# Group norm statistics and transposes of an attention kernel moved to token order, with x turned by DMA

## The chip, the cores and the metric

The kernel runs on one core of a Trainium2 chip. The metric is the device time of one execution in microseconds (us). TensorE (PE), VectorE (DVE), ScalarE (ACT), GpSimd (POOL) and SyncE (SP) run their own instruction streams in order and wait for one another through semaphores.

## The reference

x has shape 64 x 14 x 14 x 768 in fp32: 64 images of 196 tokens with 768 channels. What is computed is

```
gn    = (x - mean) / sqrt(var + 1e-5)        # per image, 32 groups of 24 channels over all 196 tokens
qkv   = gn @ qkv_w.T + qkv_b,  q += gn @ la_q.T @ lb_q.T,  v += gn @ la_v.T @ lb_v.T
attn  = softmax(q * scale @ k.T + rel_h(q) + rel_w(q))       # 12 heads of 64, per image
out   = x + (attn @ v) @ proj_w.T + proj_b
```

## The kernel before

A first block (`prepare`) loads the weights, folds the low-rank parts in, turns them on TensorE and splits each into an fp16 high and low part. The second block (`attend`) works on 32 pairs of images. A pair is 392 tokens in four tiles of 98. Products of fp32 accuracy are made of three fp16 matmuls (high x high, high x low, low x high).

All engines follow orders written out by hand: `PE_ORDER`, `ACT_ORDER`, `DVE_ORDER`, `POOL_ORDER`, `SP_ORDER`. One pass over an order is called a row of the pipeline here; in row q an entry `each(kind, old, k...)` is the step `kind` of pair q - old, so that -1 is the next pair, -2 the one after it, and 1 and 2 are earlier ones. `sequence` unrolls the orders over all rows from -2 on. A row has twelve units, each begun by S (scores of head pair k//2 of image k%2):

- Q, K, V: 18 matmuls of 392 columns each (L556) into a bank of `ring`, read by ACT (high part) and DVE (low part). Y is the same for the output projection (L623), Z turns the result back to token order on PE (L629), DVE adds x into `y_sb` (L803).
- S: scores (L599). DVE takes the row maximum (L769, L773), ACT the exponentials (N, L682), DVE and ACT scale and split them (N and T, L777, L781, L789, L690), SP turns `split` into `turned` by a DMA transpose (SP's T, L528) and `v_split` into `v_tok` (VT, L523), PE multiplies (P, L613). `S` of the next unit waits for the exponentials of the last.
- R: relative position terms (L578, L756, L762), copied by SP's CA and CB.
- X: PE turns x, fp32, from 98 tokens x 768 channels to 128 channels x 392 tokens (L637, 24 transposes for a pair); ACT copies each of the six results to `xT` (L708), DVE takes `bn_stats` of each half (L808).
- M and G: `bn_aggr` (L813, L814), a mean over the channels of each group by a matmul with `gmean` (L642), the spread of the channel means, a second matmul, and `pow` on POOL (L722).
- H and L: DVE normalises `xT` (L833), ACT writes `xn_hi` (L712), DVE `xn_lo` (L839). Q waits for `xn_lo` in three steps.
- LD: ACT's queue loads x of a later pair (L653). LY loads x again for the sum and ST stores, by way of `YS` = 3 slots of `y_sb`.

`ring` has five banks given out in the order of use (`ring_plan`): a user of a bank waits until the fifth user before it has been read. ACT and DVE begin `attend` with a wait for two memsets on POOL (L716, L717).

Of the kernel before, what the change touches and what calls it, by code (L numbers as in the profile page):

```python
# [35 lines left out]
GP = C // GROUPS // CT  # L36
# [3 lines left out]
YS = 3  # L40
# [12 lines left out]
def each(kind, old, *ks):  # L53
    return [(kind, old, k) for k in ks]
# [6 lines left out]
    + each("S", 0, 3) + each("P", 0, 1) + each("K", 0, 2) + each("Y", 1, 2) + each("Z", 1, 1)  # L61
    + each("S", 0, 4) + each("P", 0, 2) + each("V", 0, 2) + each("Z", 1, 2) + each("Q", -1, 0)
    + each("S", 0, 5) + each("P", 0, 3) + each("K", 0, 3) + each("Q", -1, 1)
    + each("S", 0, 6) + each("P", 0, 4) + each("V", 0, 3) + each("Q", -1, 2, 3)
    + each("S", 0, 7) + each("P", 0, 5) + each("K", 0, 4) + each("Q", -1, 4)
    + each("S", 0, 8) + each("P", 0, 6) + each("Q", -1, 5) + each("V", 0, 4)
    + each("S", 0, 9) + each("P", 0, 7) + each("R", -1, 0) + each("K", 0, 5) + each("R", -1, 1) + each("Y", 1, 3)
    + each("S", 0, 10) + each("P", 0, 8) + each("R", -1, 2, 3, 4) + each("V", 0, 5) + each("Y", 1, 4) + each("Z", 1, 3)
    + each("S", 0, 11) + each("P", 0, 9) + each("K", -1, 0) + each("X", -2, 0, 1, 2) + each("Y", 1, 5) + each("Z", 1, 4))


def soft(u):
# [4 lines left out]
    each("Y", 2, 5) + each("X", -1, 3) + each("N", 0, 0) + each("X", -1, 4, 5) + each("T", 0, 0)  # L77
    + each("V", 0, 0) + each("P", 1, 11) + each("N", 0, 1) + each("K", 0, 1) + each("T", 0, 1)
    + each("Y", 1, 0) + soft(2) + each("V", 0, 1)
    + each("Y", 1, 1) + each("H", -1, 0) + each("P", 0, 1) + each("N", 0, 3) + each("K", 0, 2) + each("T", 0, 3)  # L80
    + each("H", -1, 1)
    + each("Y", 1, 2) + each("H", -1, 2) + soft(4) + each("V", 0, 2)
    + each("Q", -1, 0) + each("P", 0, 3) + each("N", 0, 5) + each("K", 0, 3) + each("T", 0, 5)
    + each("Q", -1, 1) + soft(6) + each("V", 0, 3) + each("LD", -2, 0) + each("Q", -1, 2)
    + each("Q", -1, 3) + each("P", 0, 5) + each("N", 0, 7) + each("K", 0, 4) + each("T", 0, 7)
    + each("Q", -1, 4) + soft(8) + each("Q", -1, 5)
    + each("V", 0, 4) + each("P", 0, 7) + each("R", -1, 0) + soft(9) + each("K", 0, 5) + each("R", -1, 1)
    + each("Y", 1, 3) + each("R", -1, 2) + each("N", 0, 10) + each("R", -1, 3, 4) + each("T", 0, 10) + each("V", 0, 5)
    + each("Y", 1, 4) + each("P", 0, 9) + each("N", 0, 11) + each("K", -1, 0) + each("T", 0, 11)
    + each("X", -2, 0, 1, 2))  # L90
# [40 lines left out]

PER_PAIR = {"Q": 6, "K": 6, "V": 6, "R": RCH, "Y": 6, "Z": 6, "X": 6, "G": 2}
# [21 lines left out]
def build(nc, x, qkv_w, qkv_b, proj_w, proj_b, la_q, lb_q, la_v, lb_v, rel_h, rel_w, out, pairs=PAIRS):  # L154
    V, A, T, G = nc.vector, nc.scalar, nc.tensor, nc.gpsimd
    with ExitStack() as keep:
# [12 lines left out]
        gmean = sb(keep, "gmean", [128, 128], F32)  # L169
# [18 lines left out]
def prepare(nc, g):  # L188
# [5 lines left out]
    with ExitStack() as own:  # L194
# [65 lines left out]
        def _(pool):  # L260
            count = [0]

            def step(ins):
# [7 lines left out]

            step(G.memset(gmean[:, :], 1.0 / GP))
            view = gmean[:, :].rearrange("p (a b) -> p a b", b=GP)
            step(G.affine_select(out=view, in_=view, compare_op=ALU.is_ge, fill=0.0, base=0,
                                 pattern=[[-GP, 128 // GP], [0, GP]], channel_multiplier=1))
            step(G.affine_select(out=view, in_=view, compare_op=ALU.is_ge, fill=0.0, base=GP - 1,
                                 pattern=[[GP, 128 // GP], [0, GP]], channel_multiplier=-1))

# [23 lines left out]
        def _(dve):  # L302
# [76 lines left out]
            for part, table in enumerate((rt_hi, rt_lo)):  # L379
                for head in range(2):  # L380
                    for at in (32 * head, 32 * head + 16):
                        rows = slice(64 * head, 64 * head + 64)
                        V.tensor_copy(table[rows, :, :, at:at + H],
                                      rel16[rows, part, :, :].rearrange("p a (r k) -> p a r k", r=H))

        @block.tensor
        def _(pe):
# [19 lines left out]
            pe.wait_ge(pool_step, 7)  # L407
# [7 lines left out]
            for n, (grp, t, j0) in enumerate(turns):  # L415
                if n >= 4:
                    pe.wait_ge(lo_made, n - 3)
                for i in range(3):
                    if grp < 3:
                        src = stage[:, j0 + i, :].rearrange("p (a b) -> p b a", b=CT)[:, t, :]  # L420
                    else:
                        src = stage[:, j0 + i, 128 * t:128 * t + 128]
                    last = T.transpose(ring[:, n % 4, 128 * i:128 * i + 128], src, ident[:, :])
                last.then_inc(turned, 1)


def attend(nc, g, pairs):
# [9 lines left out]
    with ExitStack() as own:  # L437
        S = lambda name, shape, dt: sb(own, name, shape, dt)
        sem = lambda name: own.enter_context(nc.semaphore(name))
        xT = S("xT", [128, CT, NT], F32)  # L440
        xn_hi = S("xn_hi", [128, 2, CT, NT], F16)
        xn_lo = S("xn_lo", [128, 2, CT, NT], F16)

# [418 lines left out]
```

## Time and profile before

| | us |
|---|---|
| time, median of 3 runs | 3375.34 (3371.14 to 3375.82) |
| the profiled execution, its own time | 3373.03 |
| its span in the trace | 3371.3 |
| PE busy | 3297.2 |
| DVE busy | 2528.2 |
| ACT busy | 2098.2 |
| PE work on the chain that ended last | 94% of the span |

A matmul's duration includes its way through the array, and successive matmuls overlap, so what a group costs is read from the starts of its first matmul and of the next group's, and not from the mean. The same holds in smaller measure for DVE and ACT, where an instruction starts some 0.08 us before the last one ends. The mean granted TensorE clock of the execution was 0.991.

### The profile page before, as it was taken

What the parts mean: (1) busy time and instruction counts of PE and PEld (TensorE: products, weight loads), DVE (VectorE), ACT (ScalarE), POOL (GpSimd) and SP (SyncE); (2) the same over time, 40 slices, a digit from 0 to 9 for tenths busy, and PEclk for the clock granted to TensorE, in tenths of its full rate; (3) what the DMA queues carried; (4) which work ended last, traced back from release to release, by engine and by line L of the source; (5) the groups of instructions that cost most, each with busy time, mean ns of one, the idle gap of its engine ahead of it and who ended that gap; (6) DMA issues with size and microseconds to landing.
All of it is one profiled execution on the core that took longest, in us unless ns stands there. A gap on an engine that the chain in (4) does not pass through costs nothing.

```text
span 3371.3 us, 80148 instructions
## 1 busy us (share of the span) xinstructions
PE 3297.2 (98%) x31984; PEld 2130.7 (63%) x31984; DVE 2528.2 (75%) x5970; ACT 2098.2 (62%) x5651; POOL 35.8 (1%) x65
## 2 busy tenths in 40 slices
PE   7689999999999999999999999999999999999998
PEld 4456666666666666666666666666666666666665
DVE  7577777777777777777777777777777777777764
ACT  2466666666666666666666666666666666666664
POOL 0000000000000000000000000000000000000000
PEclk9799999999999999999999999999999999999999
DMA  3145664555555556565555555555565555565554
GB/s 128 42 96 109 120 122 103 115 113 112 118 121 107 113 112 114 116 121 107 110 116 113 112 123 118 101 117 111 110 127 120 100 118 108 111 126 122 103 106 105
DMA packets 1091412, 376.13 MB, mean 112 GB/s; under 512 B 916696, under 2 KB 1071320, under 8 KB 1091040
## 3 DMA queue, kind: packets, MB, share of 16 engines
q1 hardware_dynamic: 1075206, 333.63, 49.8%
q10 hardware_dynamic: 15834, 37.37, 3.9%
q8 instruction: 254, 4.16, 0.5%
q14 instruction: 118, 0.97, 0.1%
HBM read 86.60 MB, written 38.54 MB: 37 GB/s over the span
## 4 chain that ended last, share of the span: by engine, by line
PE 94%; DVE 2%; ACT 1%; issue 0%; DMA 0%; POOL 0%; SPq 0%; POOLq 0%; DVEq 0%
PE ring L556 51%; PE ring L623 17%; PE score L599 9%; PE o_ps L613 7%; PE ring L578 3%; PE ring L637 3%; PE ring L629 3%; ACT prob L682 1%; PE ring L642 0%; PE ring L563 0%; DVE split L789 0%; DVE row_max L769 0%; DVE rel_sb L762 0%; DVE split L781 0%; DVE rel_sb L756 0%
## 5 line engine op out<-in xcount | busy, mean ns | idle before, releaser
L556 PE MATMUL ring<-xn_hi,w_hi 128*128 128x392 f16 x3456 | 1143.2, 331 | 4.8 <-DVE xn_lo L839 4.6
L556 PE MATMUL ring<-xn_lo,w_hi 128*128 128x392 f16 x3456 | 1139.8, 330 | 0.0
L556 PE MATMUL ring<-xn_hi,w_lo 128*128 128x392 f16 x3456 | 1139.3, 330 | 0.5 <-issue 0.5
L682 ACT ACTIVATE prob<-score,neg_max,exp_scale 98x196 f32<-98x196 f32 x1536 | 769.8, 511 | 252.9 <-DVE neg_max L773 245.4
L769 DVE TENSOR_REDUCE row_max<-score 98x4 f32<-98x784 f32 x384 | 373.3, 972 | 273.2 <-PE score L599 272.1
L789 DVE SCALAR_TENSOR_TENSOR split<-prob,row_inv,split 98x196 f16<-98x196 f32 x1536 | 545.0, 417 | 7.8
L556 PEld LDWEIGHTS ring<-xn_hi,w_hi 128*128 128x128 f16 x3456 | 342.3, 99 | 260.7 <-issue 7.7
L556 PEld LDWEIGHTS ring<-xn_hi,w_lo 128*128 128x128 f16 x3456 | 338.8, 98 | 237.9 <-issue 3.6
L556 PEld LDWEIGHTS ring<-xn_lo,w_hi 128*128 128x128 f16 x3456 | 338.9, 98 | 208.3 <-issue 1.9
L623 PE MATMUL ring<-o_hi,w_hi 128*128 128x392 f16 x1152 | 380.2, 330 | 1.4 <-DVE o_lo L798 1.4
L623 PE MATMUL ring<-o_lo,w_hi 128*128 128x392 f16 x1152 | 379.8, 330 | 0.0
L623 PE MATMUL ring<-o_hi,w_lo 128*128 128x392 f16 x1152 | 379.6, 330 | 0.0
L690 ACT ACTIVATE split<-prob,row_inv 98x196 f16<-98x196 f32 x768 | 310.3, 456 | 52.9 <-DVE row_inv L777 52.1
L682 ACT ACTIVATION_READ_ACCUMULATOR prob<-score,neg_max,exp_scale 98x1 f32 x1536 | 306.2, 199 | 0.0
L658 ACT ACTIVATE q_hi<-ring,bias 128x392 f16<-128x392 f32 x192 | 112.1, 584 | 297.8 <-PE ring L556 297.8
L777 DVE RECIPROCAL row_inv<-row_sum 98x4 f32<-98x4 f32 x384 | 68.0, 177 | 290.6 <-ACT prob L682 290.6
L613 PE MATMUL o_ps<-turned,v_tok 98*64 98x196 f16 x4608 | 269.5, 252 | 4.0 <-DMA turned<-split 4.0
L701 ACT ACTIVATE yT<-ring,bias,y_scale 128x392 f32<-128x392 f32 x192 | 130.1, 678 | 220.6 <-PE ring L623 220.6
L599 PE MATMUL score<-k_hi,q_hi 64*98 64x196 f16 x1536 | 205.7, 264 | 19.7 <-DVE k_lo L736 12.3
L781 DVE TENSOR_SCALAR split<-prob,row_inv 98x196 f16<-98x196 f32 x768 | 213.0, 320 | 14.3 <-DVE row_inv L777 0.8
L613 PEld LDWEIGHTS o_ps<-turned,v_tok 98*64 98x64 f16 x4608 | 184.8, 109 | 56.1 <-DMA turned<-split 4.3
L697 ACT ACTIVATE o_hi<-o_ps,bias 128x392 f16<-128x392 f32 x192 | 112.7, 587 | 141.3 <-PE o_ps L613 141.3
(118 smaller groups left out, 4896.7 us busy)
## 6 DMA issues: line engine op xcount, KB each, us to landing
y_sb<-in_x SPq DMA_DIRECT2D x192, 196.0 KB
out<-y_sb SPq DMA_DIRECT2D x192, 196.0 KB
x_sb<-in_x ACTq DMA_DIRECT2D x31, 1176.0 KB
rel_q<-rel_sb SPq DMA_DIRECT2D x128, 122.5 KB, 2.4
stage<-in_L_conv_qkv_w SPq DMA_DIRECT2D x3, 2304.0 KB, 15.4
turned<-split SPq DMA_TRANSPOSE x384, 4.2
rel_q<-rel_sb SPq DMA_DIRECT2D x128, 24.5 KB, 1.9
v_tok<-v_split SPq DMA_TRANSPOSE x192, 3.4
```

What stands on the lines that cost most here:

```text
L556: last = T.matmul(ring[:, bank, 0:NT], w[:, c, 128 * j:128 * j + 128], xx[:, par, c, :], start=(c == 0 and part == 0), stop=(c == CT - 1 a ...
L599: last = T.matmul(score[0:HALF, head, to], stat[rows, qs], kk[rows, :], start=(part == 0), stop=(part == 3))
L613: last = T.matmul(o_ps[rows, c0:c0 + TOK], v_tok[0:HALF, hp % 2, vv, 2 * image + kh, rows], turned[0:HALF, image, pp, head, :, kh, 0:HALF] ...
L623: last = T.matmul(ring[:, bank, 0:NT], w[:, c, 128 * j:128 * j + 128], oo[:, par, c, :], start=(c == 0 and part == 0), stop=(c == HP - 1 a ...
L658: last = A.activation(to, ring[:, bank, 0:NT], ACT.Identity, bias=bias[:, j:j + 1])
L682: last = A.activation(prob[:, head, half, :], score[0:HALF, head, TOK * half:TOK * half + TOK], ACT.Exp, bias=neg_max[:, k % 2, i:i + 1], ...
L690: last = A.activation(split[0:HALF, k % 2, 0, 0, half, :, 0:HALF], prob[:, 0, half, :].rearrange("p (a k) -> p a k", a=2), ACT.Copy, scale ...
L697: A.activation(o_hi[:, par, hp, :], o_ps[:, 0:NT], ACT.Identity, bias=bias[:, 2 * CT + hp:2 * CT + hp + 1]).then_inc(o_hi_made, 1)
L701: A.activation(yT[:, k % 2, :], ring[:, bank, 0:NT], ACT.Identity, bias=bias[:, 3 * CT + k:3 * CT + k + 1], scale=y_scale[:, :]).then_inc( ...
L769: V.tensor_reduce(row_max[:, k % 2, :], score[0:HALF, :, 0:2 * TOK].rearrange("p a (b k) -> p a b k", b=2), AX.X, ALU.max).then_inc(row_ma ...
L781: last = V.tensor_scalar(split[0:HALF, k % 2, 0, 1, half, :, 0:HALF], prob[:, 1, half, :].rearrange("p (a k) -> p a k", a=2), row_inv[:, k ...
L789: last = V.scalar_tensor_tensor(split[0:HALF, k % 2, 1, head, half, :, 0:HALF], prob[:, head, half, :].rearrange("p (a k) -> p a k", a=2), ...
```

## The change

The group norm is worked out in token order (98 tokens in the partitions, channels along the free dimension), on `x_sb` itself. `A` sums x over groups (two `tensor_reduce`, each of two token tiles, 1536 elements), `G 0` is a matmul with a constant matrix that gives the mean to all partitions, `B` subtracts it in place, `U` squares on ACT, `D` sums the squares, `G 1` turns and sums them to one column of 64, POOL takes the power -0.5, `E` puts the result on a diagonal, `G 2` gives it to all partitions, `H` multiplies. `I` (ACT) and `L` (DVE) write the fp16 high and low part to `xs`, and SP turns `xs` into `xn` by four DMA transposes for a pair (`XT`). X on PE, its copies on ACT and its statistics are gone. `squares` and the `qw` buffers share the memory of `xs`. `YS` falls to 2, `yT` to one buffer, the tables of R to 32 columns, and the channel order of the weights is now the plain one. The wait of ACT and DVE for all cleared buffers is replaced by one wait for each buffer at its first use.

```diff
-YS = 3
+YS = 2
 PE_ORDER = (
-    each("S", 0, 0) + each("P", 1, 10) + each("Z", 2, 5) + each("X", -1, 3, 4, 5) + each("V", 0, 0)
-    + each("S", 0, 1) + each("P", 1, 11) + each("K", 0, 1) + each("Y", 1, 0) + each("G", -1, 0)
-    + each("S", 0, 2) + each("P", 0, 0) + each("G", -1, 1) + each("V", 0, 1) + each("Y", 1, 1) + each("Z", 1, 0)
...
+    each("S", 0, 0) + each("P", 1, 10) + each("Z", 2, 5) + each("V", 0, 0) + each("K", 0, 1)
+    + each("S", 0, 1) + each("P", 1, 11) + each("G", -1, 1) + each("V", 0, 1) + each("G", -1, 2) + each("Y", 1, 0)
+    + each("S", 0, 2) + each("P", 0, 0) + each("K", 0, 2) + each("Y", 1, 1) + each("Z", 1, 0)
+    + each("S", 0, 3) + each("P", 0, 1) + each("Y", 1, 2) + each("Z", 1, 1) + each("V", 0, 2)
+    + each("S", 0, 4) + each("P", 0, 2) + each("Z", 1, 2) + each("K", 0, 3) + each("Q", -1, 0)
...
+    + each("S", 0, 8) + each("P", 0, 6) + each("G", -2, 0) + each("Q", -1, 4, 5)
+    + each("S", 0, 9) + each("P", 0, 7) + each("K", 0, 5) + each("R", -1, 0) + each("Y", 1, 3) + each("R", -1, 1)
     + each("S", 0, 10) + each("P", 0, 8) + each("R", -1, 2, 3, 4) + each("V", 0, 5) + each("Y", 1, 4) + each("Z", 1, 3)
-    + each("S", 0, 11) + each("P", 0, 9) + each("K", -1, 0) + each("X", -2, 0, 1, 2) + each("Y", 1, 5) + each("Z", 1, 4))
+    + each("S", 0, 11) + each("P", 0, 9) + each("K", -1, 0) + each("Y", 1, 5) + each("Z", 1, 4))
 ACT_ORDER = (
+    each("Y", 2, 5) + each("U", -1, 1) + soft(0) + each("V", 0, 0)
+    + each("K", 0, 1) + each("P", 1, 11) + soft(1) + each("V", 0, 1)
+    + each("Y", 1, 0) + each("I", -1, 0) + each("N", 0, 2) + each("K", 0, 2) + each("T", 0, 2) + each("I", -1, 1)
...
+    + each("Q", -1, 0) + each("P", 0, 3) + soft(5) + each("V", 0, 3) + each("LD", -2, 0)
...
+    + each("Y", 1, 4) + each("U", -2, 0) + each("P", 0, 9) + each("N", 0, 11) + each("K", -1, 0) + each("T", 0, 11))
 DVE_ORDER = (
+    each("S", 0, 0) + each("D", -1, 1) + soft(0) + each("V", 0, 0) + each("Z", 2, 4, 5)
+    + each("S", 0, 1) + each("G", -1, 1) + each("K", 0, 1) + each("P", 1, 11) + each("E", -1, 0) + soft(1)
+    + each("G", -1, 2) + each("V", 0, 1) + each("H", -1, 0)
+    + each("S", 0, 2) + each("H", -1, 1) + each("N", 0, 2) + each("K", 0, 2) + each("T", 0, 2) + each("L", -1, 0)
+    + each("S", 0, 3) + each("Z", 1, 0) + each("P", 0, 1) + each("L", -1, 1) + soft(3)
...
+    + each("S", 0, 6) + each("Q", -1, 1) + each("N", 0, 6) + each("K", 0, 4) + each("T", 0, 6) + each("A", -2, 0)
+    + each("S", 0, 7) + each("Q", -1, 2) + each("P", 0, 5) + soft(7) + each("V", 0, 4) + each("A", -2, 1)
+    + each("S", 0, 8) + each("Q", -1, 3) + each("G", -2, 0) + soft(8) + each("Q", -1, 4) + each("B", -2, 0)
...
     + each("S", 0, 11) + each("Z", 1, 3) + each("P", 0, 9) + each("N", 0, 11) + each("K", -1, 0) + each("T", 0, 11)
-    + each("X", -2, 0, 1, 2))
+    + each("B", -2, 1) + each("D", -2, 0))
 SP_ORDER = (
     each("ST", 2, 4) + each("CB", 0, 0) + each("T", 0, 0)
-    + each("VT", 0, 0) + each("LY", 1, 0) + each("ST", 2, 5) + each("T", 0, 1) + each("LY", 1, 1)
...
+    + each("VT", 0, 0) + each("ST", 2, 5) + each("LY", 1, 0) + each("T", 0, 1)
+    + each("VT", 0, 1) + each("LY", 1, 1) + each("XT", -1, 0) + each("T", 0, 2)
+    + each("XT", -1, 1, 2) + each("ST", 1, 0) + each("XT", -1, 3) + each("T", 0, 3) + each("LY", 1, 2)
...
+                elif kind == "XT":
+                    part, image = k // 2, k % 2
+                    wait(sp, xs_lo_made if part else xs_hi_made, 2 * p + image + 1)
+                    sp.sem_inc(sp_go, 1)
+                    sp.dma_start_transpose(xn[:, p % 2, part, 2 * image:2 * image + 2].rearrange("p b c r -> p (b c) r"),
+                                           xs[0:ROWS, part, 2 * image:2 * image + 2].rearrange("r b c -> r (b c)")
+                                           ).then_inc(xn_in, 16)
...
-                        if kind == "Q" and k == 0 and c % 2 == 0:
-                            wait(pe, xn_lo_made, 3 * p + c // 2 + 1)
+                        if kind == "Q" and k == 0 and c == 0:
+                            wait(pe, xn_in, 64 * p + 64)
...
         def _(act):
-            act.wait_ge(split_zeroed, 2)
...
+                elif kind == "U":
+                    wait(act, centred, 2 * p + k + 1)
+                    if p == 0 and k == 0:
+                        act.wait_ge(xs_zeroed, 1)
+                    wait(act, done["R"], RCH * p)
+                    A.activation(squares[:, two], x_sb[:, two, :], ACT.Square).then_inc(squared, 1)
...
         def _(pool):
+            G.memset(minus_half[:, :], -0.5).then_inc(minus_half_made, 1)
+            G.memset(ones[:, :], 1.0).then_inc(ones_made, 1)
+            G.memset(xs[:, :, :, :].rearrange("p a b c -> p (a b c)"), 0.0).then_inc(xs_zeroed, 1)
+            G.memset(v_split[:, :, :, :, :].rearrange("p s a b k -> p (s a b k)"), 0.0).then_inc(v_zeroed, 1)
             G.memset(split[:, :, :, :, :, :, :].rearrange("r s a b c d k -> r (s a b c d k)"), 0.0).then_inc(split_zeroed, 1)
...
+                elif kind == "A":
+                    if k == 0:
+                        wait(dve, x_in, 16 * p + 16)
+                    two = slice(2 * k, 2 * k + 2)
+                    V.tensor_reduce(sums[:, k, :], x_sb[:, two, :].rearrange("p b (g c) -> p g b c", c=GP),
+                                    AX.XY, ALU.add).then_inc(summed, 1)
...
+                elif kind in ("B", "H"):
+                    wait(dve, read["G"], 3 * p + (1 if kind == "B" else 3))
+                    by_group = x_sb[:, 2 * k:2 * k + 2, :].rearrange("p b (g c) -> p b g c", c=GP)
+                    of = (mean if kind == "B" else rstd)[:, k:k + 1, :]
+                    V.tensor_tensor(by_group, by_group, of.unsqueeze(3).broadcast_to([HALF, 2, GROUPS, GP]),
+                                    ALU.subtract if kind == "B" else ALU.mult
+                                    ).then_inc(centred if kind == "B" else normed, 1)
```

In `prepare`, two of POOL's three instructions that make `gmean` are gone, and `rt_hi` and `rt_lo` are half as large.

## Rows read from the trace of the kernel before

**Rows 1.** The page: busy time of each engine, share of the span, instructions
```profile
PE 3297.2 (98%) x31984; PEld 2130.7 (63%) x31984; DVE 2528.2 (75%) x5970; ACT 2098.2 (62%) x5651; POOL 35.8 (1%) x65
```

**Rows 2.** Busy time by stretch, one row of the pipeline: us, each engine (instructions), PEclk, DMA share, GB/s
```profile
2090.08:2190.56 100.48, 100.48 (x995) 65.03 (x993) 76.82 (x183) 64.67 (x176) 0.69 (x1) 1.00 0.54 114
```

**Rows 3.** Timeline of PE in one row: start us, us, line, operation, tiles
```profile
2146.35 1.75 PE L637 MATMUL ring<-ident,x_sb 98*128 98x98 f32 x12
2147.93 0.33 PE L623 MATMUL ring<-o_hi,w_hi 128*128 128x392 f16 x1
...
2165.45 0.28 PE L642 MATMUL ring<-mean_var,gmean 128*128 128x2 f32 x2
2165.66 0.29 PE L599 MATMUL score<-k_hi,q_hi 64*98 64x196 f16 x2
...
2166.47 0.70 PE L613 MATMUL o_ps<-turned,v_tok 98*64 98x196 f16 x12
```

**Rows 4.** Groups by line and shape, whole execution: busy us, mean ns | idle before
```profile
L401 PE MATMUL lora_ps<-la,lbT 4*128 4x384 f32 x48 | 31.4, 849 | 9.8 <-DVE lbT L324 7.1 <-DVE stage L334 2.7
L808 DVE BATCH_NORM_STATS2 stats<-xT 128x6 f32<-128x196 f32 x384 | 112.9, 350 | 18.1 <-ACT xT L708 18.1
L839 DVE TENSOR_TENSOR xn_lo<-xT,xn_hi 128x784 f16<-128x784 f32 x96 | 87.6, 968 | 0.0
L833 DVE TENSOR_SCALAR xT<-xT,mean,rstd 128x392 f32<-128x392 f32 x192 | 83.4, 477 | 0.9 <-POOL rstd L722 0.9
L316 DVE TENSOR_REDUCE mx<-stage 128x1 f32<-128x4608 f32 x2 | 9.9, 4942 | 0.0
L712 ACT ACTIVATE xn_hi<-xT 128x784 f16<-128x784 f32 x96 | 80.9, 845 | 9.2 <-DVE xT L833 9.2
```

**Rows 5.** Timeline of DVE around the end of unit 11
```profile
2143.74 0.96 DVE L769 TENSOR_REDUCE row_max<-score 98x4 f32<-98x784 f32 x1
...
2147.13 0.18 DVE L777 RECIPROCAL row_inv<-row_sum 98x4 f32<-98x4 f32 x1 [1.04 <-ACT prob L682]
...
2148.35 1.41 DVE L789 SCALAR_TENSOR_TENSOR split<-prob,row_inv,split 98x196 f16<-98x196 f32 x4
2149.68 1.68 DVE L808 BATCH_NORM_STATS2 stats<-xT 128x6 f32<-128x196 f32 x6
```

**Rows 6.** Timeline of SP's queue in units 0 and 1: issue start us, us
```profile
2154.23 0.33 SPq L533 DMA_DIRECT2D out<-y_sb  x1
2154.67 2.43 SPq L505 DMA_DIRECT2D rel_q<-rel_sb  x4
2158.91 2.33 SPq L528 DMA_TRANSPOSE turned<-split  x1
2161.44 1.24 SPq L523 DMA_TRANSPOSE v_tok<-v_split  x1
```

**Rows 7.** The page: DMA issues, median us from issue to landing last
```profile
turned<-split SPq DMA_TRANSPOSE x384, 4.2
v_tok<-v_split SPq DMA_TRANSPOSE x192, 3.4
```

**Rows 8.** The chain of waits at the start of the main block: start us, us
```profile
89.69 3.51 POOL split L716
93.20 1.75 POOL v_split L717
...
106.18 20.75 PE ring L556 x108
...
129.36 0.16 PE ring L563
...
2098.28 9.06 PE ring L556 x54
```

**Rows 9.** Line L653, the loads of x: issue ns min/median/max, first and last start
```profile
L653 ACTq DMA_DIRECT2D x_sb<-in_x x31: 323/323/340, 115.0 to 3106.9; - x31
```

**Rows 10.** DMA from 120 to 125 us, GB/s in 40 equal slices
```profile
GB/s 295 270 270 221 98 98 49 25 0 0 0 0 0 0 0 0 0 0 0 0 0 0 0 0 0 0 0 0 0 0 0 0 0 0 0 0 0 0 0 0
```

More of the change, by code:

```diff
@@ L76 @@
 ACT_ORDER = (
[L77 to L89, printed above, removed]
@@ L270, in _ @@
                                  pattern=[[-1, 128]], channel_multiplier=1))
[L272 to L277, printed above, removed]
+            step(G.memset(gmean[:, :], 1.0 / (GP * TOK)))
             step(G.memset(pick[:, :, :], 0.0))
@@ L418, in _ @@
                 for i in range(3):
[L419 to L423, printed above, removed]
+                    last = T.transpose(ring[:, n % 4, 128 * i:128 * i + 128],
+                                       stage[:, j0 + i, 128 * t:128 * t + 128], ident[:, :])
                 last.then_inc(turned, 1)
@@ L577, in _ @@
                                             "p (g i w) -> p g i w", i=n_rows, w=W)[:, :, i, :]
-                                    last = T.matmul(cols, tab[rows, ax, row, 32 * head:32 * head + 32], mov,
+                                    last = T.matmul(cols, tab[rows, ax, row, :], mov,
                                                     start=(part == 0), stop=(part == 2))
@@ L718, in _ @@
-            G.memset(minus_half[:, :], -0.5).then_inc(minus_half_made, 1)
             pool.wait_ge(minus_half_made, 1)
             for kind, p, k in sequence(POOL_ORDER, pairs):
-                wait(pool, read["G"], 2 * p + 2)
-                G.tensor_tensor(rstd[:, :], var_eps[:, :], minus_half[:, :], ALU.pow).then_inc(rstd_made, 1)
+                wait(pool, read["G"], 3 * p + 2)
+                G.tensor_tensor(inv_dev[:, :], var_eps[:, :], minus_half[:, :], ALU.pow).then_inc(inv_dev_made, 1)
@@ new lines, in _ @@
+                elif kind == "A":
+                    if k == 0:
+                        wait(dve, x_in, 16 * p + 16)
+                    two = slice(2 * k, 2 * k + 2)
+                    V.tensor_reduce(sums[:, k, :], x_sb[:, two, :].rearrange("p b (g c) -> p g b c", c=GP),
+                                    AX.XY, ALU.add).then_inc(summed, 1)
+                elif kind == "D":
+                    wait(dve, squared, 2 * p + k + 1)
+                    two = slice(2 * k, 2 * k + 2)
+                    V.tensor_reduce(sums[:, k, :], squares[:, two].rearrange("p b (g c) -> p g b c", c=GP),
+                                    AX.XY, ALU.add).then_inc(summed, 1)
+                elif kind == "G" and k == 1:
+                    wait(dve, done["G"], 3 * p + 2)
+                    V.tensor_scalar(var_eps[:, :], ring[0:2 * GROUPS, bank, 0:1], EPS, None,
+                                    ALU.add).then_inc(read["G"], 1)
+                elif kind == "E":
+                    wait(dve, inv_dev_made, p + 1)
+                    V.tensor_scalar(diagonal[:, :], ident[0:2 * GROUPS, 0:2 * GROUPS], inv_dev[:, :], None,
+                                    ALU.mult).then_inc(diagonal_made, 1)
+                elif kind == "G":
+                    wait(dve, done["G"], 3 * p + k + 1)
+                    to = mean if k == 0 else rstd
+                    V.tensor_copy(to[:, :, :].rearrange("p n g -> p (n g)"),
+                                  ring[0:HALF, bank, 0:2 * GROUPS]).then_inc(read["G"], 1)
+                elif kind in ("B", "H"):
[5 more added lines that the diff above has]
+                                    ).then_inc(centred if kind == "B" else normed, 1)
```

195 lines of the change are left out of this document (82 added, 113 removed).

## The prediction

> **What bounds the kernel now.** I read the page's busy times first: PE 3297.2 of 3371.3 us, DVE 75% [rows 1]. A share says little, so I cut out one row of the pipeline: in the 100.48 us from one S 4 to the next PE is busy for all 100.48, DVE for 76.82, ACT for 64.67, at full clock, with the DMA engines 0.54 busy [rows 2]. In this steady part, some 30 rows, any time taken off PE is gained until another wait opens; time put on DVE costs nothing until it makes PE wait. Start and end are different: there PE waits for chains, so they are worked out apart.
>
> **PE in a steady row.** X leaves: the first twelve transposes start at 2146.35 and Y at 2147.93, so 1.58 for half a pair and 3.17 for a pair (the other half is alike) [rows 3]. The mean duration of a transpose would say twice as much; the starts count. The two G matmuls leave: 2165.45 to 2165.66 is 0.21 each, 0.42 together [rows 3]. Three come. G 1 has one column: 0.21. G 0 and G 2 have 64 columns, in fp32, which takes two instructions; L401 shows 31.4/48 = 0.654 us for 384 columns, 1.70 ns a column [rows 4], so 0.21 + 62 x 1.70 x 2 ns = 0.42 each. Together 1.05; no row shows this form, so the bounds are 0.63 (columns hidden) and 1.7 (twice the column price and a cold array). I take 1.05. The sum for a pair: -3.17 - 0.42 + 1.05 = -2.54. The moving operand of Q, K, V now lies in four runs of 98 instead of one of 392; P already reads runs of 98 at its normal pace, so nothing. Some 29.5 pairs have their X on a full PE (pair 0 and half of pair 1 fall in the start): **-75 us**, bounds -67 to -87.
>
> **DVE in a steady row.** Passes of 98 x 1536: the reduction of 4608 takes 4.94 and L839, with 784, takes 0.97 [rows 4], so 1.04 ns an element and 0.97 + 0.78 = 1.75, of which the next instruction hides some 0.08: 1.7. There are ten (A, B, D, H, L two each): 17.0, and 0.6 for G and E. Out go the statistics (112.9/32 = 3.5), H (83.4/32 = 2.6), L (87.6/32 = 2.7) [rows 4] and about 1.4 of aggregates and small steps: 10.2. So 76.8 + 7.4 = 84 of 98. ACT: U and I, 1536 elements, four times 0.85 + 0.63 = 1.48 by L712 [rows 4], 5.9 in and as much out. Neither is the bound by its sum; what matters is the order.
>
> **Where DVE can make PE wait.** A unit costs PE 0.81 for S and 0.63 for P, so 1.5 with the changeover, and 9.06/3 = 3.02 for each group of 18 matmuls [rows 8]. From the start of the maximum to the end of the exponentials is 2147.13 - 2143.74 = 3.4 [rows 5], so S of the next unit, 7.3 to 8.1 later, leaves DVE some 3 us of lateness for nothing. I went through the new orders unit by unit with these prices.
> - Unit 10: the four R steps (7 us of DVE) end with V 5 some 1.7 after S 11 starts.
> - Unit 11: max, Z, P, N, K, T end at S 11 + 7.8; then B 1 and D 0, at the end of the row, 11.2. PE needs 8.1 for the unit, so DVE enters the next row 3.1 late, the maximum of S 0 runs to 4.2, the exponentials to 6.5. S 1 is due at 8.1: no wait.
> - Unit 0: D 1 lies under the exponentials (ready at 5.9), then N, T, V, and Z 4 at 9.7, Z 5 at 10.3. PE reaches V 1 at 9.8, whose bank is that of Z 4: no wait, by 0.1. G 2 waits for E (pow on POOL 0.75 behind G 1): E is done at S 1 + 4.7, just when PE has finished V 1.
> - SP: ST 4 stands ahead of CB, T 0 and VT 0. Before, Z 4 was read 2.6 after S 0, and ST left at 2154.23; CB takes 2.43, T 0 was issued at 2158.91, VT 0 at 2161.44 [rows 6], with P 0 at 2166.47 [rows 3]. Now ST 4 leaves at 9.7, CB ends at 12.6, T 0 is issued to 14.2 or 15.0 (1.5, or the 2.33 of this row), VT 0 lands 3.4 later [rows 7], at 17.5 to 18.4. P 0 is due at 2 x 8.1 + 0.8 = 17.0. So **P of unit 0 waits for `v_tok`**, 0.4 to 1.4; I take 0.8. For 30 rows **+24 us**, bounds 0 (DVE 1 us earlier than I think) and 2 a row.
> - Units 2 and 3: H 0, I 0, H 1, I 1, L 0, L 1 end at S 3 + 5.5. XT lies between VT and T in size (12 blocks of 128 columns against 8 and 16), so 3.8 to land; the fourth lands near S 3 + 9.5, Q 0 is due at S 3 + 13.2. XT 0 stands ahead of T 2 on SP, but I 0 is early. No wait, by some 3.7.
> - Unit 6: LD is issued 2 us before S 6 and needs 6 (below); A 0 comes at S 6 + 6.9, cover 2 to 3. If it is gone, S 7's maximum, queued behind A 0, still has 3 us.
>
> The Trainium skill, in "VectorE: DVE Perf Modes", section "The three transpose paths", gives 1309 ns for a 128x128 block turned by DMA and 390 ns on TensorE, and advises TensorE where PSUM will do as the target. It speaks against this change. The rows do not bear the figure out: `turned`, sixteen blocks, lands 4.2 us after its issue [rows 7], where the page would make it 21.
>
> **The start.** Before, POOL's memset of `split` begins at 89.69, and ACT and DVE wait for it and the next one; Q starts at 106.18 [rows 8]. Now the first pair's chain is serial: from 89.7 A A 3.4; G 0 with a cold array and its copy 1.2; B B 3.4; D D 3.4 (U beside them); G 1, epsilon, pow, E, G 2, copy 3.2; H H L L 6.8; the last XT 1.0 + 3.8 to land: 115.9. That is +9.7. The wait that goes is worth nothing: `xs`, 6144 elements at 3.51/4096 us, is clear at 95.2, the first U is due at 96.1. Then Q to R, 23.2 before (129.36 - 106.18): G 0 of pair 1 now stands between Q 3 and Q 4, and wants its x. LD was issued at 115.0 [rows 9] and its data ended near 121.0 [rows 10], 6 us. Now it goes at Q + 5.7, x is there at Q + 12.0, A, Q 2, A end at 16.5, Q 5 is done at 23.1, R starts at 25.5: +2.3. The first full row lacks P, Y and Z of earlier pairs and was held by DVE and by two places where PE did two or three jobs in one unit; by the same sums it falls from 95.7 to 88.1: -7.6, of which -12 to 0 is possible. Two instructions less on POOL before the first DVE step: -1.2. Together **+3 us**, bounds -8 to +15.
>
> **The end.** With two slots of `y_sb`, Z 2 of the last pair waits for ST 0 to land and LY 2 after it, and Z 5 for ST 3: some 3 us each beyond PE's pace, the last one seen in full. **+3 us**, bounds 0 to 6.
>
> **The sum.** -75 + 24 + 3 + 3 = -45 against 3373.03, the profiled execution: 3328. The median of the runs shown is 2.3 higher: 3330.
>
> **The rivals.**
> 1. No new wait: Z 4 is read a microsecond earlier, or `v_tok` lands sooner. For it: the margins at V 1, G 2 and P 0 are all within 1 us, less than my error over twenty steps. -75 + 6: 3304.
> 2. The waits of units 0 to 2 are larger, 1.3 to 2.2 a row, as lateness of DVE adds to all three. For it: D, B and A are forms of which no row shows one (four dimensions, runs of 24). 3304 + 30 x 1.3 to 2.2 = 3343 to 3370. Against: DVE idles 14% of the row and catches up by unit 4.
> 3. Slower: B and H, whose two inputs are both fp32 in SBUF, one of them a broadcast, run at half the pace, 3.3 instead of 1.7. The nearest row, L839, has an fp32 and an fp16 input at 1.04 ns an element and speaks against it. Then Z 4 comes at 11.3: V 1 waits 1.5, P 0 another 0.9, Q 0 some 0.6: 3.0 a row, 3304 + 90 = 3394. It decides from a wait of 2.2 a row on; any lateness of DVE of that size does the same.
> 4. The crossbar turns `xs` slowly. It would work through `xn_in`: by [rows 7] the longest median is 4.2 for sixteen blocks, and Q 0 has 3.7 us of cover beyond 3.8; at 10 us to land, more than twice any row here, Q 0 waits 2.5 a row, 3304 + 75 = 3379. By the figure of the Trainium skill, "VectorE: DVE Perf Modes", "The three transpose paths", twelve blocks would land after 15.7 us, an estimate that the row above denies.
>
> **How the numbers follow.** My forecast 0.40; rival 1 0.25; rival 2 0.20; rival 3 0.13; rival 4 0.02. A measurement of this kernel can tell 0.2%, about 7 us, from no change, so "same" is 3368 to 3382. Faster: 0.40 + 0.25 + 0.17 = 0.82; same 0.05 (the end of rival 2 and part of 4); slower 0.13. The range takes in the forecast and rivals 1 and 2 with the bounds of start and price of G: 3290 to 3368, leaving out 0.17.
>
> **What would show it.** A row of the pipeline 98.7 long (97.9 without the new wait); no PE line for x; G at 1.0 a pair; ten DVE passes near 1.7; DVE 84 a row; PE's o_ps waiting for `v_tok` once a row, some 0.8; Q's first matmul at 115 to 116, and no steady wait on `xn`; the last Z behind LY. I am wrong if the passes take much over 1.7, or if PE waits for `xn` or for exponentials in every row.

## The result, and the profile after

The kernel after the change takes 3381.8 us (median, 3373.48 to 3395.74) beside 3374.54 for the kernel before: a ratio of 1.0025, 95% interval 1.0018 to 1.0033. It is slower by a quarter of a per cent, where 3330 and a gain of 1.3% were forecast. The profiled execution spans 3380.6 us, 9.3 more than before.

The page of after, busy times, answers [rows 1]:

```profile
PE 3218.0 (95%) x31280; PEld 2005.9 (59%) x31280; DVE 2755.3 (82%) x5490; ACT 2125.4 (63%) x5491; POOL 35.2 (1%) x65
```

PE does 79.2 us less and the kernel is no faster: PE now waits. Where it waits is in PE's waits from 1000 to 3000 us, twenty rows of the pipeline (us in total, times, longest us):

```profile
PE o_ps L611 <- issue: 20.0, 18, 3.7
PE o_ps L611 <- DMA turned<-split: 15.2, 8, 2.8
PE ring L554 <- DVE y_sb L815: 3.9, 11, 0.4
PE ring L639 <- DVE sums L821: 3.3, 20, 0.2
```

The busy time by stretch of after, columns as in [rows 2], two thousand microseconds of the steady part, then 8.2 us behind the longest wait, 7.1 us behind a wait of 2.05 and 8.3 us behind one of 2.69:

```profile
1000.00:2000.00 1000.00, 976.26 (x9665) 609.94 (x9665) 834.24 (x1670) 650.62 (x1687) 5.42 (x10) 0.99 0.65 127
2000.00:3000.00 1000.00, 979.77 (x9707) 612.39 (x9704) 838.77 (x1680) 655.16 (x1700) 5.41 (x10) 1.00 0.66 128
...
1973.80:1978.00 4.20, 4.14 (x22) 2.31 (x23) 0.89 (x4) 0.84 (x4) 0.00 (x0) 0.50 1.02 222
1978.00:1982.00 4.00, 4.00 (x21) 2.14 (x20) 0.91 (x3) 1.53 (x4) 0.00 (x0) 0.79 0.25 55
...
2076.90:2084.00 7.10, 7.09 (x52) 4.36 (x52) 5.11 (x11) 5.08 (x13) 0.00 (x0) 1.00 1.00 209
...
2775.70:2784.00 8.30, 8.26 (x41) 4.49 (x42) 2.70 (x7) 3.27 (x12) 0.00 (x0) 0.63 0.82 179
```

The two lines of `o_ps` (L611) make 35.2 us in twenty rows. 32.2 of them are P of unit 0, 1.61 a row, where 0.8 was forecast; the other 3.0 are six waits at P 10 of the pair before, just behind S 0; waits of that kind stay when P of unit 0 no longer waits (below). From one row maximum of S 0 to the next, 29 rows took 2915.9 us before (241.89 to 3157.82) and 2907.1 after (256.17 to 3163.26): 100.55 and 100.24 a row. The steady part gained 0.31 a row instead of 1.8; the start, up to the first of these maxima, lost 14.3; what comes behind the last of them lost 3.9. -8.8 + 14.3 + 3.9 = +9.4, the 9.3 of the spans but for rounding.

One ordinary row and the worst one, PE's timeline of after (start us, us, the wait ahead in brackets, with what ended it), answering [rows 3]:

```profile
1420.13 0.36 PE L639 MATMUL ring<-sums,gmean 98*98 98x64 f32 x2 [0.17 <-DVE sums L821]
...
1453.85 0.29 PE L597 MATMUL score<-k_hi,q_hi 64*98 64x196 f16 x2
...
1463.76 0.50 PE L554 MATMUL ring<-xn,w_hi 128*128 128x392 f16 x2 [0.36 <-DVE y_sb L815]
...
1472.70 0.70 PE L611 MATMUL o_ps<-turned,v_tok 98*64 98x196 f16 x12 [1.58 <-DMA turned<-split]
...
1973.86 1.19 PE L611 MATMUL o_ps<-turned,v_tok 98*64 98x196 f16 x12 [3.68 <-issue]
```

SP's queue ahead of the P at 1472.70, answering [rows 6], and DVE's reading of Z 4 and Z 5 that lets ST 4 go:

```profile
1463.72 0.33 SPq L531 DMA_DIRECT2D out<-y_sb  x1
1464.17 2.43 SPq L496 DMA_DIRECT2D rel_q<-rel_sb  x4
1466.71 1.55 SPq L519 DMA_TRANSPOSE turned<-split  x1
1468.45 1.84 SPq L514 DMA_TRANSPOSE v_tok<-v_split  x1
```

```profile
1457.01 0.96 DVE L779 TENSOR_REDUCE row_max<-score 98x4 f32<-98x784 f32 x1
...
1463.02 1.28 DVE L815 TENSOR_TENSOR y_sb<-ring,y_sb 98x512 f32<-98x512 f32 x2
```

Against S 0 at 1453.85 the steps read: DVE takes the maximum at +3.2, Z 4 is read at +9.8, ST 4 leaves at +9.9, CB is through at +12.75, T 0 is issued at +12.9, VT 0 at +14.6, P starts at +18.85 and would have started at 17.3. The bracket names `turned`; it and `v_tok` are both awaited there, and both stand behind ST 4 on SP. By the trace T 0 landed at 1471.83 and VT 0 at 1472.61, 0.09 before P began, so `v_tok` is what P waited for.

The second price is in the last four rows of the stretches. Behind the wait of 3.68 PE ran 4.2 us at a granted clock of 0.50, that is 1.2 GHz, and the twelve P matmuls took 1.19 instead of 0.70. Rows with a wait near 1.1 are 99.3 long; the row with 3.68 is 104.7 long (1956.06 to 2060.74), so 2.6 us of wait more made the row 5.4 longer. Six of the 29 rows take 101.9 to 104.7: their waits at P are 1.97 to 3.68, and behind each of them a stretch stands below full clock. The others take 97.9 to 100.4; two of these have a wait of 2.05 and kept the full clock (the stretch from 2076.90).

### The profile page after: what moved, and what is told of

Read it like the earlier page. It is cut to its first block, busy times and chain, and to the rows that moved or that the text cites. A ratio compares the mean times of both kernels' runs of the same rounds, so it can differ in the third digit from the quotient of the medians.

```text
span 3380.6 us, 78578 instructions
## 1 busy us (share of the span) xinstructions
PE 3218.0 (95%) x31280; PEld 2005.9 (59%) x31280; DVE 2755.3 (82%) x5490; ACT 2125.4 (63%) x5491; POOL 35.2 (1%) x65
## 4 chain that ended last, share of the span: by engine, by line
PE 57%; DVE 23%; ACT 9%; issue 4%; DMA 4%; SPq 2%; POOL 0%; ACTq 0%; DVEq 0%; POOLq 0%
PE ring L554 31%; PE ring L621 11%; ACT prob L686 6%; DVE split L801 6%; PE score L597 5%; PE o_ps L611 4%; DVE sums L821 3%; DMA turned<-split 3%; DVE row_max L779 2%; PE ring L576 2%; DVE x_sb L845 2%; DVE split L793 2%; PE ring L627 2%; DVE rel_sb L772 1%; DVE sums L826 1%
## 5 line engine op out<-in xcount | busy, mean ns | idle before, releaser
L554 PE MATMUL ring<-xn,w_hi 128*128 128x392 f16 x6912 | 1720.6, 330 | 17.7 <-DMA xn<-xs 11.8
L554 PE MATMUL ring<-xn,w_lo 128*128 128x392 f16 x3456 | 1137.7, 329 | 0.0
L554 PEld LDWEIGHTS ring<-xn,w_hi 128*128 128x128 f16 x6912 | 645.5, 97 | 493.2 <-issue 14.1
L554 PEld LDWEIGHTS ring<-xn,w_lo 128*128 128x128 f16 x3456 | 333.1, 96 | 246.1 <-issue 6.1
L611 PE MATMUL o_ps<-turned,v_tok 98*64 98x196 f16 x4608 | 270.8, 252 | 55.0 <-DMA turned<-split 29.4
L611 PEld LDWEIGHTS o_ps<-turned,v_tok 98*64 98x64 f16 x4608 | 187.0, 109 | 108.6 <-DMA turned<-split 33.6
L597 PE MATMUL score<-onehot,rel_q 64*98 64x196 f16 x1536 | 191.4, 245 | 0.0
L597 PE MATMUL score<-k_lo,q_hi 64*98 64x196 f16 x1536 | 191.3, 245 | 0.0
L597 PE MATMUL score<-k_hi,q_lo 64*98 64x196 f16 x1536 | 191.1, 245 | 0.0
```

The lines of the kernel that those rows point to most:

```text
L554: last = T.matmul(ring[:, bank, 0:NT], w[:, c, 128 * j:128 * j + 128], xn[:, par, xx, :, c, 0:HALF], start=(c == 0 and part == 0), stop=(c ...
L597: last = T.matmul(score[0:HALF, head, to], stat[rows, qs], kk[rows, :], start=(part == 0), stop=(part == 3))
L611: last = T.matmul(o_ps[rows, c0:c0 + TOK], v_tok[0:HALF, hp % 2, vv, 2 * image + kh, rows], turned[0:HALF, image, pp, head, :, kh, 0:HALF] ...
```

## The experiments

**One order on SP.** T 0 and VT 0 go ahead of ST 4 and CB; nothing else of the kernel after changes.

```
-    each("ST", 2, 4) + each("CB", 0, 0) + each("T", 0, 0)
-    + each("VT", 0, 0) + each("ST", 2, 5)
+    each("T", 0, 0)
+    + each("VT", 0, 0) + each("ST", 2, 4) + each("CB", 0, 0) + each("ST", 2, 5)
```

> The changed kernel with SP's row begun by T 0 and VT 0, with ST 4 and CB behind them. Queue theory (P of unit 0 waits because ST 4, now late, holds CB, T 0 and VT 0 back on SP): T 0 and VT 0 are issued as soon as unit 0 is split, some 3 us earlier, PE's wait for o_ps and the cold stretch behind it go, a row falls from 100.24 to some 97.7 us and the kernel to about 3306. Crossbar theory (the four more transposes of a pair slow v_tok and turned down, whatever stands ahead of them): the wait stays within 0.5 us of what it is, 3370 or more.

Measured: 3323.13, ratio 0.9855 (0.984 to 0.987). PE's waits from 1000 to 3000 us:

```profile
PE ring L554 <- DVE y_sb L815: 4.5, 13, 0.4
PE ring L639 <- DVE sums L821: 3.7, 21, 0.2
PE o_ps L611 <- issue: 1.5, 5, 0.4
```

The wait at `o_ps` falls from 35.2 to 1.5, PE is busy for 1989.5 of 2000 us, and a row takes 98.19 (1339.42 to 1437.61). The 1.5 are all waits of that P 10: P of unit 0 didn't wait once. The order of SP's queue alone holds 57 us (1.0025 against 0.9855). The transposes themselves, XT among them, are unchanged here, so a slow crossbar isn't the cause. The time is 17 above the queue theory's 3306. That number took rows of 97.7, and the 29 rows take 98.21 on average, which is 15 of the 17.

**The same from DVE's side.** SP keeps its order, Z 4 is read ahead of D 1.

```
-    each("S", 0, 0) + each("D", -1, 1) + soft(0) + each("V", 0, 0) + each("Z", 2, 4, 5)
+    each("S", 0, 0) + each("Z", 2, 4) + each("D", -1, 1) + soft(0) + each("V", 0, 0) + each("Z", 2, 5)
```

> The changed kernel with Z 4 moved on DVE from the end of unit 0 to just behind its row maximum, ahead of D 1; SP's order untouched. Queue theory: ST 4 leaves some 4.5 us earlier, the wait for o_ps goes as in the reordered queue, about 3306. Theory that DVE's fullness (84 us a row) is what PE waits for: its work is the same, only its order differs, so most of the wait stays, 3360 or more.

Measured: 3315.61, ratio 0.9833 (0.9818 to 0.9848). DVE and SP of one row (the maximum of S 0 is at 1434.36, S 0 itself at 1431.21):

```profile
1435.49 0.69 DVE L815 TENSOR_TENSOR y_sb<-ring,y_sb 98x512 f32<-98x512 f32 x1
```

```profile
1436.20 0.33 SPq L531 DMA_DIRECT2D out<-y_sb  x1
1436.64 2.47 SPq L496 DMA_DIRECT2D rel_q<-rel_sb  x4
1440.07 1.55 SPq L519 DMA_TRANSPOSE turned<-split  x1
1441.81 1.80 SPq L514 DMA_TRANSPOSE v_tok<-v_split  x1
```

ST 4 leaves 5.0 after S 0 instead of 9.9, VT 0 is issued at +10.6 instead of +14.6, and P of unit 0 doesn't wait in any of the twenty rows; the 1.8 us left at `o_ps` are waits of P 10. V 1 no longer waits for the bank of Z 4 either (3.9 in twenty rows before this edit, none now). A row is 97.74 (1336.62 to 1434.36) and 97.93 on average over the 29, 2.6 less than before the change; DVE does all its new passes, 855 of 1000 us. So DVE's greater load costs nothing here; its order did.

**The same wait put into the kernel before.** ST 4 also waits until DVE has read V 0 of the row.

```
                 elif kind == "ST":
                     wait(sp, read["Z"], 6 * p + k + 1)
+                    if k == 4 and p + 2 < pairs:
+                        wait(sp, read["V"], 6 * (p + 2) + 1)
```

> The kernel before with one more wait: ST 4 on SP also waits until V 0 of the row has been read, some 6 us later than Z 4. No DMA transpose is added and DVE does the same work. Queue theory: VT 0 goes out near 2166 instead of 2161.4, lands 3 to 4 us after P of unit 0 is due, and 30 rows pay that and a cold clock behind it: 3374 + 100 to 190, 3474 to 3564. Crossbar theory and DVE theory: no change, within 10 us of the kernel before.

Measured: 3490.93, ratio 1.0353 (1.0335 to 1.037). PE's waits and busy time from 1000 to 3000 us:

```profile
PE o_ps L615 <- DMA turned<-split: 32.1, 12, 3.2
PE o_ps L615 <- issue: 15.5, 7, 2.5
```

```profile
1000.00:2000.00 1000.00, 975.80 (x9571) 627.14 (x9570) 735.98 (x1740) 621.33 (x1677) 6.41 (x9) 0.99 0.55 109
```

The path from ST 4 to P is the same in the kernel before, without x turned by DMA and with DVE 74% busy. Neither of the other two theories allows this: both forecast no change. A row takes 104.18 on average over the 29 (102.6 to 107.1 from the second on), 3.6 more than in before. Of these 2.4 are PE's wait at P of unit 0; the other 1.2, by subtraction, is the same work done more slowly behind the waits. It isn't spread evenly. In 12 rows the granted clock stayed full, and they are longer by their wait alone; in 16 the clock fell (0.968 to 0.984 over the row), and they are 1.7 to 3.3 longer beyond their wait. The length of the wait doesn't tell them apart: waits of 2.10 to 2.62 are in the first group, 2.14 to 3.48 in the second, and the same wait of 2.15 stands in a row of 102.66 and in one of 105.81.

**Two transfers moved off VT 0's heels.** The wait varies from row to row between 0.8 and 3.7, and I suspected ST 5 and LY 0, 196 KB each, issued right behind VT 0.

```
-    + each("VT", 0, 0) + each("ST", 2, 5) + each("LY", 1, 0) + each("T", 0, 1)
-    + each("VT", 0, 1) + each("LY", 1, 1)
+    + each("VT", 0, 0) + each("T", 0, 1)
+    + each("VT", 0, 1) + each("ST", 2, 5) + each("LY", 1, 0) + each("LY", 1, 1)
```

> The kernel after, with one change of SP's order: ST 5 (196 KB out) and LY 0 (196 KB in), which SP issues 1.9 and 2.6 us behind VT 0, go behind T 1 and VT 1. ST 4 still stands ahead of CB, T 0 and VT 0, so P of unit 0 can start no earlier than in the best rows of after. Queue theory alone (the wait is the time at which VT 0 is issued, and the scatter from 1.1 to 3.7 comes from elsewhere): P(0,0) waits 1.76 a row as in after, 3382 (3376 to 3387). Queue plus crowding (the two bulk transfers issued behind VT 0 share the DMA engines with it, and this makes it land up to 6.4 instead of 3.8 us after its issue; behind a long wait PE's clock falls): the wait is 1.1 in every row, no row runs at 1.2 GHz, rows of 99.2 instead of 100.2, 30 x 0.9 = 27 less: 3355 (3348 to 3362).

Measured: 3387.86, ratio 1.0044 (1.0028 to 1.0061). The waits from 1000 to 3000 us:

```profile
PE o_ps L611 <- issue: 19.1, 17, 2.0
PE o_ps L611 <- DMA turned<-split: 15.9, 7, 2.7
```

35.0 against 35.2 (33.8 against 32.2 for P of unit 0 alone), and the time is just above the 3376 to 3387 of the first theory: the two transfers aren't what makes the landing scatter. The traces show what goes with it. These are lines of the DMA view of after from T 0's issue to its landing, with VT 0's time to landing, in the row with the wait of 3.68 (1965.76 to 1971.79) and, behind the dots, in one with a wait of 1.09 (1367.38 to 1371.51):

```profile
q14 instruction: 1, 0.01, 1.7%
q8 instruction: 1, 0.02, 1.0%
v_tok<-v_split SPq DMA_TRANSPOSE x1, 6.3
...
q1 hardware_dynamic: 2411, 0.63, 77.9%
v_tok<-v_split SPq DMA_TRANSPOSE x1, 3.7
```

In the second stretch the queues that the profile names `instruction` move nothing. In 28 rows of after, T 0 lands 4.11 to 4.22 us after its issue in the 14 in which no packet of these queues starts while it is under way, and 4.66 to 6.34 in the 14 with one or two (8 or 16 KB each); VT 0 lands behind T 0 each time. In e5 the same split gives 4.09 to 4.19 and 4.38 to 6.29. So the lateness is there at T 0 already, ahead of ST 5 and LY 0. No run took these packets away: that they are the cause isn't shown. The scatter matters only where VT 0 is issued late: with either order edit P of unit 0 waited in none of the twenty rows.

**The start: cleared buffers.** In the kernel before, each cleared buffer is waited for at its first use, and `minus_half` and `v_split` are cleared ahead of `split`.

```
-            act.wait_ge(split_zeroed, 2)
-            dve.wait_ge(split_zeroed, 2)
...
+            G.memset(minus_half[:, :], -0.5).then_inc(minus_half_made, 1)
+            G.memset(v_split[:, :, :, :, :].rearrange("p s a b k -> p (s a b k)"), 0.0).then_inc(v_zeroed, 1)
+            G.memset(split[:, :, :, :, :, :, :].rearrange("r s a b c d k -> r (s a b c d k)"), 0.0).then_inc(split_zeroed, 1)
```

> The kernel before with one part of the change alone: each cleared buffer is waited for at its first use, and split is cleared last. ACT's first copy of x no longer waits until 94.98 but for PE alone, near 91. If the start is one serial chain, it shortens by about 4 us, 3370; if something else ends later in the start, 0.

Measured: 3373.65, ratio 1.0002 (0.9993 to 1.0011): nothing. POOL's timeline shows why:

```profile
91.24 3.52 POOL L721 MEMSET split<- 112x4096 f16 x1
101.75 0.73 POOL L725 TENSOR_TENSOR rstd<-var_eps,minus_half 128x2 f32<-128x2 f32 x1 [7.00 <-issue]
```

The last step of the statistics began at 97.24, 4.4 earlier than in before, but POOL's pow began 7.0 behind its last memset all the same. The kernel after has this too, and its memsets are 5.2 longer:

```profile
95.24 3.51 POOL L729 MEMSET split<- 112x4096 f16 x1
105.61 0.59 POOL L733 TENSOR_TENSOR inv_dev<-var_eps,minus_half 64x1 f32<-64x1 f32 x1 [6.86 <-issue]
```

Its operand was ready at 99.95. So pow comes 5.7 late, and clearing `xs` (5.2 of POOL's time) costs the start some 5.2 of it, by way of POOL and not by the wait at U, where I had looked.

**Pow ahead of two memsets.** From here on with Z 4 ahead of D 1.

```
-            G.memset(v_split[:, :, :, :, :].rearrange("p s a b k -> p (s a b k)"), 0.0).then_inc(v_zeroed, 1)
-            G.memset(split[:, :, :, :, :, :, :].rearrange("r s a b c d k -> r (s a b c d k)"), 0.0).then_inc(split_zeroed, 1)
...
                 G.tensor_tensor(inv_dev[:, :], var_eps[:, :], minus_half[:, :], ALU.pow).then_inc(inv_dev_made, 1)
+                if p == 0:
+                    G.memset(v_split[:, :, :, :, :].rearrange("p s a b k -> p (s a b k)"), 0.0).then_inc(v_zeroed, 1)
+                    G.memset(split[:, :, :, :, :, :, :].rearrange("r s a b c d k -> r (s a b c d k)"), 0.0).then_inc(split_zeroed, 1)
```

> Z 4 ahead of D 1 on DVE (the edit that gave 3315.6), and on POOL the clearing of v_split and split moved behind the pow of the first pair. In three kernels POOL's first pow began 6.9 to 7.0 us behind its last memset, though its operand was there 5.6 us before in the kernel after. Theory: these 7 us are a cost of POOL's first arithmetic instruction, counted from the end of the memsets. Then pow starts at 93.5 + 6.9 = 100.4 instead of 105.6, Q 0 at 113.6 instead of 118.8, all that follows 5 us earlier: 3310.5 (3308 to 3313). Rival: the 7 us have nothing to do with the memsets but with a fixed time after the start (about 101.8 or 105.6), then 0 to 3.8 are gained: 3312 to 3316.

Measured: 3315.59, ratio 0.983 (0.9815 to 0.9844), the time that the DVE order alone gave. Pow moved as expected, to 100.51, before the earliest time of the rival (101.8), and the gain vanished one step on. POOL's timeline, then DVE's:

```profile
100.51 0.59 POOL L731 TENSOR_TENSOR inv_dev<-var_eps,minus_half 64x1 f32<-64x1 f32 x1 [6.93 <-DVE var_eps L831]
101.07 1.79 POOL L733 MEMSET v_split<- 128x2048 f16 x1
102.82 3.50 POOL L734 MEMSET split<- 112x4096 f16 x1
```

```profile
101.14 5.23 DVE L835 TENSOR_SCALAR diagonal<-ident,inv_dev 64x64 f32<-64x64 f32 x1 [1.15 <-POOL inv_dev L731]
```

The scaling that makes `diagonal` takes 0.25 elsewhere; here it ends at 106.38, with POOL's second memset at 106.32.

**The memsets behind that scaling.** One wait of POOL more.

```
                 if p == 0:
+                    pool.wait_ge(diagonal_made, 1)
                     G.memset(v_split[:, :, :, :, :].rearrange("p s a b k -> p (s a b k)"), 0.0).then_inc(v_zeroed, 1)
```

> The kernel e6_pow_first with one wait more: POOL begins to clear v_split and split only when DVE has written diagonal (E of the first pair). In e6_pow_first pow came at 100.51 as expected, but DVE's scaling of ident by inv_dev, 64 x 64 and 0.25 us in every other kernel, took 5.23 us, from 101.14 to 106.38, beside POOL's two memsets, which ran from 101.07 to 106.32, and nothing was gained. Theory (the two engines share a path to SBUF, and this DVE form, fp32 from SBUF to SBUF with a scalar, doesn't get it while a memset runs): with the memsets behind it the scaling takes 0.25 again, G 2 goes at 101.5, Q 0 at 113.5, and all that follows 5.1 earlier: 3310.4 (3308 to 3313). H and L (two fp32 inputs) then run beside the memsets, as B did beside the memset of xs at 1.7 each, and are not held. Rival A: the 5 us are a first-use cost of the scaling or of its scalar operand that merely lay hidden before, independent of the memsets: 3315.6. Rival B: H is held in its turn: 3315.6 with H 5 us longer.

Measured: 3308.96, ratio 0.9813 (0.98 to 0.9826), the fastest of all. DVE's timeline, then PE's:

```profile
100.88 0.25 DVE L836 TENSOR_SCALAR diagonal<-ident,inv_dev 64x64 f32<-64x64 f32 x1 [1.13 <-POOL inv_dev L731]
101.87 0.22 DVE L841 COPY rstd<-ring 98x64 f32<-98x64 f32 x1 [0.74 <-PE ring L643]
102.13 3.43 DVE L847 TENSOR_TENSOR x_sb<-x_sb,rstd 98x1536 f32<-98x1536 f32 x2
```

```profile
113.53 0.83 PE L554 MATMUL ring<-xn,w_hi 128*128 128x392 f16 x2 [11.69 <-DMA xn<-xs]
```

The scaling takes 0.25 again, Q 0 starts at 113.53 instead of 118.63, and the H passes beside the memset of `split` take 3.43 for two, as always. Both rivals fall.

## Why the prediction was wrong, point by point

**PE's removal: right, a little small.** -2.54 a pair was forecast. With Z 4 early the 29 rows take 97.93 on average, of which 0.29 are waits: 97.64 of work against 100.49, -2.9. G costs less than I took. G 0, priced at 0.42, holds PE for 0.19 (the next matmul starts at 1420.32, behind 1420.13), and by the same reading of starts the three of a pair take 0.66 instead of 1.05. One bound of this term was wrong in itself: 1.7 for G makes -1.89 a pair and -56 us, not -67.

**DVE: right.** Passes of 1.74 to 1.75, 83.4 to 83.9 us in 100, and no wait for `xn` in a steady row. The lateness was right too: Z 4 read at +9.8 and ST 4 at +9.9 (forecast 9.7), CB through at +12.75 (12.6), P due at +17.3 (17.0).

**The failed step: the wait of P in unit 0, forecast 0.8 a row.** Two terms of it were mis-sized.
- From VT 0's issue to P I took the median landing of `v_tok`, 3.4 [rows 7]. In after it is 3.8 in the median row, 4.25 in the row shown above, 6.4 in the worst and 4.2 on average. The wait is 1.1 in the good rows and 1.61 on average. The median was 0.4 short, which goes with 1.1 for 0.8; most of the other half microsecond is the late landings, which a median leaves out.
- The clock. I priced a wait at its own length. Over the 29 rows the terms add up as -2.9 for PE, +1.5 at P of unit 0, +0.1 at P 10, +0.2 at V 1, +0.2 at G 0 and +0.1 at R, which is -0.8; measured is -0.3. Most of the missing 0.5 a row is in the six rows with a lowered clock: beyond their wait they are 1.4 to 3.0 us longer than the others, 12 us in all, 0.4 a row. The kernel before with ST 4 held back shows the same in 16 of its rows: 2.4 of waits and 1.2 of slow work a row, on average.

Together, the late Z 4 cost 2.3 a row (100.24 against 97.93 with Z 4 early) and not 0.8: 67 us in 29 rows instead of 24. The rest of the steady part is as forecast, -76 us (97.93 against 100.55) for -75. So 43 from the late Z 4, 1 less from that rest, 11 from the start and 1 from the end make 54, the miss between the spans (+9.3 for -45). Undoing the lateness gave 65 us by DVE's order and 57 by SP's, by the ratios. Rival 2 had the mechanism, 1.3 to 2.2 a row from lateness of DVE, but left out the clock and stopped at 3370; rival 4's 3379 is nearer, and its mechanism, slow turning of `xs`, didn't happen; rival 3 said that any lateness of 2.2 a row turns the sign, and this happened without slow passes. I gave the two 0.33 together and let the range stop at 3368, inside the first of them.

**The start: +3 forecast, +14.3 measured.** This is the second term that was mis-sized. Q 0 at 118.77 was forecast at 115.9: pow waited for POOL, 7 us behind memsets lengthened by `xs`, a term I had set at nothing after checking only who waits for `xs` itself. Q to R took 24.9 (forecast 25.5). The largest miss is row 0, forecast 7.6 shorter and measured 0.5 shorter (95.17 against 95.69). PE's timeline of after:

```profile
180.82 0.40 PE L597 MATMUL score<-k_hi,q_hi 64*98 64x196 f16 x2 [3.44 <-ACT prob L686]
188.43 0.28 PE L597 MATMUL score<-k_hi,q_hi 64*98 64x196 f16 x2 [1.46 <-ACT prob L686]
...
251.69 0.40 PE L597 MATMUL score<-k_hi,q_hi 64*98 64x196 f16 x2 [6.82 <-DVE k_lo L746]
```

I had counted the waits of this row away. Less work on PE in a row whose softmax and R steps bind it only lets PE wait longer: 12.4 us of waits in it, against 11.1 before.

**The end: +3 forecast, +3.9 measured, for another reason mostly.** The number is close by luck. PE's timeline behind the last row's start:

```profile
3302.02 0.29 PE L597 MATMUL score<-k_hi,q_hi 64*98 64x196 f16 x2 [0.92 <-ACT prob L686]
3308.02 0.29 PE L597 MATMUL score<-k_hi,q_hi 64*98 64x196 f16 x2 [1.41 <-ACT prob L686]
3313.96 0.29 PE L597 MATMUL score<-k_hi,q_hi 64*98 64x196 f16 x2 [1.35 <-ACT prob L686]
3319.97 0.40 PE L597 MATMUL score<-k_hi,q_hi 64*98 64x196 f16 x2 [4.51 <-ACT prob L686]
```

These 8.2 us stood at 4.5 before. Of the two slots of `y_sb` DVE's timeline shows the last Z waiting 1.67 for its load, 0.35 for PE before. I tested neither by a run.

**Crossbar: right.** `xn` lands 3.9 after its issue, the median of 128 (forecast 3.8). That is a quarter of the 15.7 us estimated in the prediction from the figure in the Trainium skill, "VectorE: DVE Perf Modes", "The three transpose paths".

## What to carry to other kernels

A tight margin behind a queue isn't priced by the median of a landing or by the length of the wait: take the spread of the landings at that place, and look row by row whether PE came back at full clock. When work moves to an engine with room, look at what the late instruction releases: here one output store, urgent for nobody, stood in SP's queue ahead of the two transposes that PE needed, and either of two order edits turned +0.25% into -1.5 or -1.7%. At the start follow every instruction of each queue to its last consumer: a memset for one buffer delayed an unrelated pow.

## What the runs showed of the hardware

- POOL's first arithmetic instruction, the pow, began 6.9 to 7.5 us behind the memset ahead of it in all nine kernels, however long its operand had been there (101.92 - 94.98 in before, 105.61 - 98.75 in after, 101.75 - 94.76 with the waits moved, 100.51 - 93.58 with pow ahead of two memsets). In before the operand came only 0.16 earlier, so that kernel alone would show nothing. What passes in these microseconds no row shows. The Trainium skill, "GPSIMD Engine Reference", "Instruction dispatch", puts about 6 us on the first call of a freshly loaded kernel on this engine; whether it is that, no run here shows.
- A DVE scaling of 64 x 64 fp32 from SBUF to SBUF took 5.23 instead of 0.25 us while POOL's memsets ran, and ended 0.06 behind them; reductions and passes with two tensor inputs ran beside memsets at 1.7 each. The Trainium skill, "SBUF — State Buffer", "SBUF: two separate sides", describes a port pair of DVE and GpSimd that one of them holds exclusively, for certain DVE forms and for whole instructions; the trace agrees, except that DVE stayed shut out over two memsets in a row.
- A transpose by DMA issued behind another (VT 0 behind T 0 in after) landed between 3.6 and 6.3 us after its issue at the same place of the row, and moving 392 KB of transfers away from it changed nothing. The one ahead of it landed in 4.11 to 4.22 us in the rows without a packet of the `instruction` queues in its time, and in 4.66 to 6.34 in the rows with one.
- The same wait of PE cost its own length in one row and 3 us more in another of the same kernel: 2.15 us in rows of 102.66 (granted clock 1.00) and 105.81 (0.968), in the kernel before with ST 4 held back.
